# V projected for two units at a time from high and low parts, with 256 columns a matmul, and rotary tables loaded anew for each layer

## The reference, cut to what matters

```python
def attn_layer(x, Wqkv, qs, ksc, Wo):
    qkv = x @ Wqkv                       # 16 heads of 64 for each of q, k, v
    q, k, v = jnp.split(qkv, 3, -1)
    q = l2norm(q) * qs
    k = l2norm(k) * ksc
    q = q * cos * scale + rotate_half(q) * sin * scale
    k = k * cos * inv + rotate_half(k) * sin * inv
    out = local_attention(q, k, v)       # windows of 32 tokens, each sees itself and the one before
    return out @ Wo

def ffn_layer(x, g, bln, W1, b1, W2, b2):
    xn = (x - mu) / jnp.sqrt(var + 1e-05) * g + bln
    a, gate = jnp.split(xn @ W1 + b1, 2, -1)
    return a * gelu(gate) @ W2 + b2
```

## Time and profile before

| | |
|---|---|
| runs | 1273.89, 1274.28, 1277.31 us; median 1274.28 |
| profiled execution | 1272.33 us |
| its span, first to last instruction | 1270.5 us |
| share of the span busy: TensorE, VectorE, ScalarE, GpSimd | 90%, 75%, 67%, 51% |
| mean granted clock of TensorE | 0.954 of full speed |
| the stack's first projection; the last projection | at 394.15 us; at 1201.24 us |
| one layer's period in the middle (step 12 to step 12) | 137.60 us |

### The profile page before, as it was taken

One profiled execution on the slowest core, in us unless ns is written; L12 is line 12 of the kernel. 1 busy time (PEld: TensorE's weight loads), 2 busy tenths in 40 slices (PEclk: granted clock), 3 DMA queues, 4 the chain that ended last, 5 costly groups with the idle time before them and its releaser, 6 DMA issues. The chain is left out here.

```text
span 1270.5 us, 26317 instructions
## 1 busy us (share of the span) xinstructions
PE 1138.3 (90%) x9636; PEld 720.2 (57%) x9636; DVE 949.0 (75%) x1399; ACT 847.5 (67%) x1356; POOL 650.1 (51%) x522
## 2 busy tenths in 40 slices
PE   7787869999765899999999999999999999999976
PEld 2222337777422576666656676666666666667541
DVE  2789957777465778787878788877878787878733
ACT  4553536665335588777877788678877787777844
POOL 1555723444323675664657465655566465756510
PEclk9888979999786899999999999999999999999997
DMA  3000007110200454344525453435434453534310
GB/s 113 1 1 0 1 17 217 51 50 1 77 24 19 97 155 99 93 123 107 133 74 129 103 134 88 112 102 134 99 98 123 109 126 76 126 90 120 87 49 17
DMA packets 75510, 107.11 MB, mean 84 GB/s; under 512 B 25347, under 2 KB 31938, under 8 KB 75002
## 3 DMA queue, kind: packets, MB, share of 16 engines
q1 hardware_dynamic: 75386, 105.47, 31.9%
HBM read 30.89 MB, written 0.59 MB: 25 GB/s over the span
## 5 line engine op out<-in xcount | busy, mean ns | idle before, releaser
L1680 POOL TENSOR_TENSOR st_sq_sum<-h 128x512 f32<-128x512 f32 x96 | 123.5, 1287 | 250.0 <-ACT h L1426 249.4
L1563 DVE SCALAR_TENSOR_TENSOR st_turned<-banks,mo_w 128x1024 f32<-128x1024 f32 x96 | 117.6, 1225 | 74.6 <-ACT banks L1437 43.2
L1426 ACT ACTIVATE h<-banks 128x512 f32<-128x512 f32 x192 | 112.1, 596 | 68.2 <-PE banks L1269 64.9
L1684 POOL TENSOR_TENSOR mo_w<-mo_w,x 128x512 f32<-128x512 f32 x96 | 122.5, 1276 | 61.4 <-DVE x L1549 60.5
L1330 PEld LDWEIGHTS banks<-st_p_blocks,st_vs 128*64 128x64 f32 x1536 | 81.8, 138 | 78.6 <-issue 74.6
L1289 PEld LDWEIGHTS banks<-st_wv,stream 128*128 128x128 f32 x768 | 100.6, 191 | 45.4 <-issue 44.7
L1686 POOL TENSOR_TENSOR mo_w<-mo_w,x 128x512 f32<-128x512 f32 x96 | 122.4, 1275 | 0.0
L1277 PE MATMUL banks<-st_sq_sum,head_ones 128*128 128x512 f32 x192 | 103.3, 620 | 16.1 <-POOL st_sq_sum L1680 16.1
L1458 ACT ACTIVATE st_p_blocks<-banks 64x512 f32<-64x512 f32 x192 | 112.2, 584 | 3.2 <-PE banks L1318 0.8
L430 POOL TENSOR_TENSOR ma_dbx<-ma_u,ma_b_rows 128x1024 f32<-128x1024 f32 x32 | 75.4, 2360 | 75.8 <-ACT ma_b_rows L288 51.9
L1693 POOL TENSOR_TENSOR mo_w<-st_prob,st_ri 128x512 f32<-128x512 f32 x96 | 100.2, 1044 | 15.2 <-DVE st_ri L1651 15.2
(11 more groups left out here) (234 smaller groups left out, 2780.1 us busy)
## 6 DMA issues: line engine op xcount, KB each, us to landing
st_qT<-st_turned SPq DMA_DIRECT2D x192, 128.0 KB, 2.4
st_k_blocks<-st_turned SPq DMA_DIRECT2D x384, 64.0 KB, 2.0
st_vs<-st_vn SPq DMA_DIRECT2D x96, 192.0 KB, 2.5
st_w_raw<-in_w_qk SPq DMA_DIRECT2D x12, 512.0 KB, 4.7
st_vs<-st_vn SPq DMA_DIRECT2D x96, 48.0 KB, 2.1
mo_w_all<-gate_rows SPq DMA_DIRECT2D x1, 3072.0 KB, 12.9
st_wv<-in_w_v SPq DMA_DIRECT2D x12, 256.0 KB, 3.0
st_wo<-in_wo SPq DMA_DIRECT2D x12, 256.0 KB, 3.0
```

The source lines that it names most:

```text
L1426: A(sq[:, part, :], ps[:, part, :], ACT.Square).then_inc(sq_done.sem, 1)
L1563: v.scalar_tensor_tensor(turned[:, h % 4], NORM_BANK.unsqueeze(1).to_broadcast([P, 2, SEQ]), 1e12, cos_part[:, which], ALU.min, ALU.mult). ...
L1680: nc.gpsimd.tensor_tensor(sq_sum[:], sq[:, 0, :], sq[:, 1, :], ALU.add).then_inc(sq_summed.sem, 1)
L1684: nc.gpsimd.tensor_tensor(cos_part[:, which, 0, :], cos_part[:, which, 0, :], sin_part[:, 1, :], ALU.subtract).then_inc(add_done.sem, 1)
```

## The change

- **V in two parts, two units at a time.** V's weights are loaded as fp32 into `wv_raw`, 4 pieces of 256 columns, and split like those of Q and K. One call of `project_v` now makes half of the token tiles (two of four) for a pair of units, with three fp32r matmuls of 256 columns for each tile, from `y_high` and `y_low`. It runs a step earlier (for t + 2), so that both halves of a pair are there when its first unit needs them. `vn` and `vs` hold a pair; the shift is issued on odd steps, for both units at once.
- **More pieces to split.** 12 pieces a layer instead of 8, by a table: one each in steps 5, 6, 7, 9, 11 and 14, two in steps 8, 10 and 12, none in 13; in the first layer V's pieces are split in steps -3, -1, 1 and 3. GpSimd's part stays ahead of its other work in the first layer's early steps and behind it else. A V piece waits until the last use of the old one.
- **Tables.** `table` is gone. In step 2 SyncE loads 4 x 512 KB of tables for the next layer straight into `scaled`, and ScalarE scales them in place in steps 4 to 7. V's weights come in one load in step 3 instead of two loads in steps 11 and 15.
- **Smaller buffers.** `turned` has 3 buffers instead of 4, `rn` one instead of two, `dsq` shares `rstd`'s place.

```diff
-        self.w_raw, self.wv, self.wo = sb("w_raw", [P, 8, 2 * P]), sb("wv", [P, 8, P]), sb("wo", [P, 8, P])
-        self.rope_scale, self.table = sb("rope_scale", [P, 4]), sb("table", [P, 4, SEQ])
+        self.w_raw, self.wv_raw, self.wo = sb("w_raw", [P, 8, 2 * P]), sb("wv_raw", [P, 4, 2 * P]), sb("wo", [P, 8, P])
+        self.rope_scale, self.scaled = sb("rope_scale", [P, 4]), sb("scaled", [P, 2, 2, 2, 2, SEQ])
...
-    def load_v(self, sp, d, layer, half):
-        pairs = slice(4 * half, 4 * half + 4)
-        sp.dma_start(self.wv[:, pairs, :], at_layer(d["w_v"], layer)[:, pairs, :]).then_inc(self.wv_in[half].sem, 16)
+    def load_v(self, sp, d, layer):
+        sp.dma_start(self.wv_raw[:], at_layer(d["w_v"], layer)).then_inc(self.wv_in.sem, 16)
...
+    def load_tables(self, sp, d, layer):
+        for which in range(2):
+            for part in range(2):
+                sp.dma_start(self.scaled[:, layer % 2, which, :, part, :], d["rope"][:, 2 * which:2 * which + 2, :]).then_inc(self.table_in.sem, 16)
...
-    turned = sb("turned", [P, 4, 2, SEQ])
+    rn = sb("rn", [P, SEQ])
+    turned = sb("turned", [P, 3, 2, SEQ])
...
+    SPLITS = PARTS + PARTS // 2
+
+    PIECES = "q0 q1 q2 v0 q3 q4 v1 q5 q6 v2 q7 v3".split()
+    PIECES_AT = (5, 6, 7, 8, 8, 9, 10, 10, 11, 12, 12, 14)
+    FIRST_AT = (-5, -4, -3, -3, -2, -1, -1, 0, 1, 1, 2, 3)
+
+    def qk_split(i):
+        return PIECES.index(f"q{i}") + 1
+
+    def v_split(g):
+        return PIECES.index(f"v{g}") + 1
+
+    def pieces_of(s, t):
+
+        first = [(piece, 0) for piece, at in zip(PIECES, FIRST_AT) if s.first and at == t]
+        return first + [(piece, 1) for piece, at in zip(PIECES, PIECES_AT) if not s.last and at == t]
...
         def shift_values(s, n):
-            r = n % 2
-            sp.wait_ge(*v_copied.at(s.turn, n + 1))
+            r = n // 2 % 2
+            sp.wait_ge(*v_copied.at(s.turn, n + 2))
             sp.dma_start(vs[32:128, r, :, :], vn[0:96, r, :, :]).then_inc(vs_in[r].sem, 16)
             sp.dma_start(vs[0:32, r, 1:4, :], vn[96:128, r, 0:3, :]).then_inc(vs_in[r].sem, 16)
...
-                if t >= -1 and s.unit(t + 1):
+                if t >= -1 and t % 2 == 1 and s.unit(t + 1):
...
+                    if t == 2:
+                        if product_done.any(turn, 0):
+                            sp.wait_ge(*product_done.at(turn, 0))
+                        places.load_tables(sp, d, turn + 1)
                     if t == 3:
 
-                        sp.wait_ge(*w_split.at(turn, PARTS))
+                        sp.wait_ge(*w_split.at(turn, SPLITS))
                         for half in range(2):
                             places.load_qk(sp, d, turn + 1, half)
+                        places.load_v(sp, d, turn + 1)
                         sp.wait_ge(*scaled_done.at(turn, 4))
                         places.load_scale(sp, d, turn + 1)
-                    if t == 11:
-                        sp.wait_ge(*v_done.at(turn, 12))
-                        places.load_v(sp, d, turn + 1, 0)
                     if t == 13:
                         sp.wait_ge(*wo_step.at(turn, 12))
                         places.load_wo(sp, d, turn + 1, 0)
-                    if t == 15:
-                        sp.wait_ge(*v_done.at(turn, 16))
-                        places.load_v(sp, d, turn + 1, 1)
...
         def project_v(s, n, job, stage):
 
-            b, pair = n // 8 % 2, n % 8
+            b, g, half = n // 8 % 2, n % 8 // 2, n % 2
             if v_copied.any(s.turn, n):
                 pe.wait_ge(*v_copied.at(s.turn, n))
             if stage in (2, 3):
                 pe.wait_ge(*act_done.at(s.turn, 3 * job + stage))
-            pe.wait_ge(*wv_in[pair // 4].at(s.turn, 16 * (n // 16) + 16))
-            for tile in range(4):
-                rows = slice(P * tile, P * tile + P)
-                last = mm(V_BANK[:, rows], Y[:, b, rows], wv[:, pair, :], start=True, stop=True)
+            if n % 16 < 8 and half == 0:
+                pe.wait_ge(*w_split.at(s.turn, SPLITS * (n // 16) + v_split(g)))
+            if n % 8 == 0:
+                pe.wait_ge(*y_low_done.at(s.turn, n // 8 + 1))
+            for i in range(2):
+                rows = slice(P * (2 * half + i), P * (2 * half + i) + P)
+                out = V_BANK[:, 2 * P * i:2 * P * i + 2 * P]
+                mm(out, y_high[:, b, rows], wv_high[:, g, :], start=True, stop=False)
+                mm(out, y_high[:, b, rows], wv_low[:, g, :], start=False, stop=False)
+                last = mm(out, y_low[:, b, rows], wv_high[:, g, :], start=False, stop=True)
             last.then_inc(v_done.sem, 1)
...
         def values(s, n):
-            r = n % 2
-            pe.wait_ge(*vs_in[r].at(s.turn, 32 * (n // 2) + 32))
+            r, q = n % 2, n // 2 % 2
+            pe.wait_ge(*vs_in[q].at(s.turn, 32 * (n // 4) + 32))
...
-                if t >= -1 and s.unit(t + 1):
-                    project_v(s, t + 1, job, stage)
+                if t >= -2 and s.unit(t + 2):
+                    project_v(s, t + 2, job, stage)
...
-            if ahead and product_done.any(s.turn, 0):
-                ac.wait_ge(*product_done.at(s.turn, 0))
+            ac.wait_ge(*table_in.at(s.turn, 64 * ahead + 64))
             col = 2 * which + part
-            A(scaled[:, (s.turn + ahead) % 2, which, :, part, :], table[:, 2 * which:2 * which + 2, :], ACT.Copy, scale=rope_scale[:, col:col + 1]).then_inc(scaled_done.sem, 1)
+            A(scaled[:, (s.turn + ahead) % 2, which, :, part, :], scaled[:, (s.turn + ahead) % 2, which, :, part, :], ACT.Copy, scale=rope_scale[:, col:col + 1]).then_inc(scaled_done.sem, 1)
...
         def copy_v(s, n):
-            r = n % 2
+            r, half = n // 2 % 2, n % 2
             ac.wait_ge(*v_done.at(s.turn, n + 1))
-            if pv_done.any(s.turn, n - 1):
-                ac.wait_ge(*pv_done.at(s.turn, n - 1))
-            if vs_in[r].any(s.turn, 32 * (n // 2)):
-                ac.wait_ge(*vs_in[r].at(s.turn, 32 * (n // 2)))
-            A(vn[:, r], V_BANK.rearrange("p (j f) -> p j f", f=P), ACT.Copy).then_inc(v_copied.sem, 1)
+            if half == 0:
+                if pv_done.any(s.turn, n - 2):
+                    ac.wait_ge(*pv_done.at(s.turn, n - 2))
+                if vs_in[r].any(s.turn, 32 * (n // 4)):
+                    ac.wait_ge(*vs_in[r].at(s.turn, 32 * (n // 4)))
+            A(vn[:, r, 2 * half:2 * half + 2, :], V_BANK.rearrange("p (j f) -> p j f", f=2 * P), ACT.Copy).then_inc(v_copied.sem, 1)
...
-        def high_weights(s, i, ahead):
-
-            dv.wait_ge(*proj_in.at(s.turn, 32 * ahead + 32))
-            v.tensor_copy(w_high[:, i, :], w_raw[:, i, :]).then_inc(w_high_done.sem, 1)
+        def high_weights(s, piece, ahead):
+
+            i = int(piece[1])
+            if piece[0] == "q":
+                dv.wait_ge(*proj_in.at(s.turn, 32 * ahead + 32))
+                v.tensor_copy(w_high[:, i, :], w_raw[:, i, :]).then_inc(w_high_done.sem, 1)
+            else:
+                dv.wait_ge(*places.wv_in.at(s.turn, 16 * ahead + 16))
+                if ahead:
+                    dv.wait_ge(*v_done.at(s.turn, 10 + 2 * i))
+                v.tensor_copy(wv_high[:, i, :], wv_raw[:, i, :]).then_inc(w_high_done.sem, 1)
...
+            last = g - 2 + which
             for pair in range(2):
-                if heads_in[g % 2][pair].any(s.turn, HEADS_IN * (g // 2)):
-                    dv.wait_ge(*heads_in[g % 2][pair].at(s.turn, HEADS_IN * (g // 2)))
-            v.scalar_tensor_tensor(turned[:, h % 4], NORM_BANK.unsqueeze(1).to_broadcast([P, 2, SEQ]), 1e12, cos_part[:, which],
+                if heads_in[last % 2][pair].any(s.turn, HEADS_IN * (last // 2 + 1)):
+                    dv.wait_ge(*heads_in[last % 2][pair].at(s.turn, HEADS_IN * (last // 2 + 1)))
+            v.scalar_tensor_tensor(turned[:, (UNITS * s.turn + h) % 3], NORM_BANK.unsqueeze(1).to_broadcast([P, 2, SEQ]), 1e12, cos_part[:, which],
...
-                if s.first and t + 5 < PARTS:
-                    high_weights(s, t + 5, 0)
-                if t >= PARTS - 1 and t < 2 * PARTS - 1 and not s.last:
-                    high_weights(s, t - PARTS + 1, 1)
+                for piece, ahead in pieces_of(s, t):
+                    high_weights(s, piece, ahead)
...
-        def low_weights(s, i, ahead):
-            pool.wait_ge(*w_high_done.at(s.turn, PARTS * ahead + i + 1))
-            nc.gpsimd.tensor_tensor(w_low[:, i, :], w_raw[:, i, :], w_high[:, i, :], ALU.subtract).then_inc(w_split.sem, 1)
+        def low_weights(s, piece, ahead):
+
+            i = int(piece[1])
+            low, raw, high = (w_low, w_raw, w_high) if piece[0] == "q" else (wv_low, wv_raw, wv_high)
+            pool.wait_ge(*w_high_done.at(s.turn, SPLITS * ahead + PIECES.index(piece) + 1))
+            nc.gpsimd.tensor_tensor(low[:, i, :], raw[:, i, :], high[:, i, :], ALU.subtract).then_inc(w_split.sem, 1)
 
         def body(s):
             for t in s.range:
```

(12 more changed lines are left out.)

58 lines of the change are left out of this document (30 added, 28 removed).

## The result

The changed kernel takes 1281.6 us (median of 19 runs, 1274.93 to 1286.62), the kernel before 1273.89 beside it; the ratio is 1.0068 (95% interval 1.0049 to 1.0087). It is slower by about 8.7 us by the ratio; the medians lie 7.7 apart. The forecast was 1269.5, with a range of 1262 to 1279.

A forecast was written before the change was run, and what follows sets the result against it. TensorE, busy for 90% of the span, was taken as the bound in most steps. The profiled 1272.33 - 7.2 (six layers) + 2.4 (start) = 1267.5 us, 1269.5 on the scale of the runs' median; range 1262 to 1279.

The forecast's parts named there:

- price of V: V block in each step: six matmuls at 0.124 us, 0.74 for 0.89 before, a gain of 0.15 to 0.16.
- the start: Start of the stack: four V pieces split ahead of GpSimd's sum of squares cost 2.4 us once (bounds 0.7 and 3.5).
- steps 12 to 15: End of a layer: the new table of pieces gains 0.3 us for the four steps together (0 to 0.64).
- the CASTs of steps 5 to 11: Extra CASTs of weight pieces in these steps, costed at nothing: VectorE and GpSimd have idle time in the plain step.
- I cost it at nothing, at most 0.5 a layer: Tables, 2 MB a layer in step 2: about 10 us of loading inside steps 2 and 3, at no cost.
- steps 4 to 6: TensorE would come 0.48 us earlier but wait for K's transfers again; 0.2 a layer counted as gain.
- TensorE is the limit and no wait behind the V block: Steps 1, 2, 9, 10 and 7: each shortens by 0.16 us, 0.80 a layer.
- The lock rival: Steps 5 to 7: GpSimd's sum starts first and blocks the CAST; a layer gains only 0.4, 1274 to 1275; chance 0.28.
- The load rival: V block: weight loads are not hidden behind the streams, 1.28 us, 0.39 more than now; 1300; chance 0.06.
- the full gain: V matmuls at 0.107 us, K's transfers in time: ten steps a layer gain 0.25 each; 1262; chance 0.10.
- I am wrong if layers after the first don't shorten: Failure sign: the layer's period should fall from 137.6 to about 136.3 us.
- the ring: VectorE and GpSimd loop without TensorE, 7.19 us in steps 12 to 14; as rival in all steps 1278.5, chance 0.09.

The follow-up runs named there:

- e12: e9 with layer 1's QK weights (1 MB) loaded in step 2 of layer 0 instead of step 3; ratio 0.9955 to the kernel before.
- e1: The kernel before with only the tables reloaded for each layer (2 MB in step 2), V as it was; ratio 1.0070 to the kernel before.
- e2: The changed kernel with layer 1's tables loaded ahead of the stack, none in step 2 of layer 0; ratio 1.0060 to the kernel before.
- e5: e3 with the next layer's V weights loaded in step 4 behind K's transfers instead of step 3; ratio 1.0013 to the kernel before.
- e3: e2 with GpSimd's V subtractions behind its sum of squares and additions in steps -3, -1, 1, 3 of layer 0; ratio 1.0046 to the kernel before.
- e4: e3 without the product of y_high and V's low weights, four V matmuls a step instead of six; ratio 1.0031 to the kernel before.
- e7: e5 with the five feed-forward loads issued in step 6 behind K's transfers instead of step 5; ratio 0.9981 to the kernel before.
- e8: e7 with one weight piece in each of steps 11 to 14 instead of two in step 12; ratio 0.9998 to the kernel before.
- e9: e7 with QK weight loads no longer waiting for the last V piece, only the last QK piece; ratio 0.9985 to the kernel before.
- e6: The changed kernel with V's weights loaded in step 4 behind K's transfers, tables left in step 2; 1279.12 us in one run.
- e10: e9 with the head norm reading half of the squares, not waiting for GpSimd's sum (result differs); ratio 0.9842 to the kernel before.

## Why the prediction was wrong

The mechanism that the forecast was built on held. Its price of V was right (0.117 to 0.121 us a matmul for 0.124), the start cost 2.06 us for 2.4, steps 12 to 15 gained 0.22 a layer for 0.3, and the CASTs of steps 5 to 11 cost little (step 5 of e12 takes 6.93 in layers 1 to 4 and 6.87 in layer 5, which splits no weights). Two other steps of it failed. From the forecast's -4.8 to the stack's +9.25 there are 14.05 us:

- **"I cost it at nothing, at most 0.5 a layer"** (the tables): +10.3 us in steps 4 to 6 of layer 0, three quarters of the miss. The argument placed the 2 MB "inside steps 2 and 3, of which the second alone is as long as step 11, 11.55". That is true of layers 1 to 5. In layer 0 steps 0 to 7 carry no feed-forward work, which the forecast itself used two paragraphs earlier, and steps 2 and 3 are 7.51 and 6.94 us. It also took the table load's 5.0 us, measured as the first of the stack's loads, with none ahead of it (in the changed kernel each quarter of the 2 MB took 6.4 in the median), and didn't lay the 1.5 MB of weights of step 3 and K's transfers of step 4 end to end with it. It named the shift of V, due in step 4, as what queues behind, and TensorE waited for that 3.19 us; K's transfers, behind the weights, it did not name here, and they cost 4.40. e1, e2, e5 and e12 show this, and that it takes more than one load: the tables alone make a step 4 of 13.2 us, what step 3 issues without them 11.7 to 14.6 (e2, e3, e4), QK weights and V's shift alone still 9.2 to 11.7 (e5, e7, e8, e9), and only with the QK weights a step earlier as well is the stall gone. How the 8.9 divide among these is not settled: moving V's weights alone did nothing (e6), and V's shift, twice as large, was not taken back to 240 KB in any run.

- **"TensorE is the limit and no wait behind the V block"** (steps 1, 2, 9, 10, 7, and 4 to 6): 0.80 a layer was counted for the first five, and they gave 0.02 less than nothing, 0.14, 0.08, 0.16 and 0.09, 0.45 in all. For steps 4 to 6, 0.2 was counted and 0.14 lost in layer 2, 0.16 of it in step 6, which waited for K's transfers. Over the six layers, layer 0's steps 4 to 6 and its start aside, 3.1 us were gained for 7.0. A busy share of 6.94 of 6.94 said that TensorE never idled, not by how much it missed idling. The margin was in the rows: in step 5 GpSimd's sum ends at 740.56 + 1.28 = 741.84, 3.64 us after the step's start, and one step later the norm starts at 749.04, 3.90 after its step's start. So 0.26 of margin, of which V's 0.15 and the sum's 0.07 (1.35 for 1.28, with the CAST just ahead of it) leave next to nothing. TensorE then waits a few hundredths and loses more than that, as the norm takes 1.05 from a standstill for 0.95: the 0.15 is eaten. (In step 6, where K's transfers are in time, 0.08 of it is left: 6.86 for 6.94.) e4 (another 0.24 off V: next to nothing in steps 1, 5, 6, 7 and 9) and e10 (the sum taken away: 6.78) show both halves of it.

- **The lock rival** is refuted by rows. In step 5 the CAST starts 0.08 ahead of GpSimd's sum (748.22), as the earlier trace rows let one expect, and takes 0.28, as it does in steps 6 and 7 of every layer that splits weights:

```profile
748.14 0.28 DVE L1567 CAST st_w_high<-st_w_raw 128x256 fp32r<-128x256 f32 x1
```

The Trainium skill's rule (SBUF — State Buffer, "SBUF: two separate sides") says that whoever starts first holds the shared port pair and the other waits; the trace agrees with the order (the CAST undisturbed at 0.28, the sum 1.35 for 1.28), though the sum lost only 0.07 where the two overlap by 0.20. The load rival (1300) and the full gain (1262) fall with the 0.12. "I am wrong if layers after the first don't shorten": layers 1 to 4 do, by 0.05 to 1.02, 0.5 on average. In its picture of the kernel before one row was misread: step 8 takes 9.82, not 9.42, which changes nothing in the sum.

- Of the chances, slower had 0.16, and all of that stood on V and on the ring. No rival had the transfers of layer 0 as its mechanism, though the text had named the queue. That is the gap: a load was costed by a layer in the middle, and the first layer, where steps 0 to 7 are shorter, was not looked at.

## What to carry to other kernels

Cost an added load in the shortest steps that it falls in, not in a typical layer, and lay it end to end with the transfers issued behind it up to the first that is due. A DMA share near 0.9 did no harm in a step in which nothing behind the loads was due (e12, step 3); with small urgent transfers behind them it cost 6 to 9 us (e1, the changed kernel). A busy engine is a bound only up to the slack of the next input: before counting a shorter job as gain, take for each step the difference between when the operand of the following instruction is ready and when it is read. In a first layer, order the prefetches by due time (e12), even if the other layers can stay as they are.

## What the runs showed of the hardware

- A wait of TensorE that lasts hundredths costs about 0.1 more: the head norm (two records) took 0.95 us to the next matmul in a running stream and 1.05 where it starts 0.06 behind the end of the sum that it waited for.
- An idle stretch of TensorE is paid twice: around the waits of 3.19 and 4.40 us the granted clock fell from 1.00 to 0.50, with a mean of 0.75 in that step and of 0.86 in the next, and the same scores took 1.93 us for 1.08. In e1, with waits of 1.88 and 3.41, it was 0.85.
- 64 KB transfers inside the chip, 2.0 us to landing in the median of the kernel before, took 7.9 in step 4 of layer 0 with tables, Q's transfers, V's shift and 1.5 MB of weights issued ahead of them in 12 us, at 226 to 272 GB/s (3.2 there before the change, 2.0 in e12). The length of that step varies by some 2.5 us between profiles of the same instructions.
- CASTs that run into GpSimd's sum (0.68 to 0.91 us for 0.28) were cheaper in one heap than spread: three steps with one CAST each took 29.43 us with the step behind them (e8), and two, none and one 29.15 (e7).
